# Three operations in place of four in each Newton round of the inverse root

## The reference

```
m = mean(x);  v = var(x)
layernorm(x) = (x - m) / sqrt(v + 1e-5)          # eight times
x = x + tanh(g) * part(layernorm(x), ...)
```

## Time and profile before

| | us |
|---|---|
| three timed executions | 1701.8, 1703.4, 1709.1 (median 1703.42) |
| the profiled execution | 1699.4 |
| its span, first to last instruction | 1697.6 |
| busy: PE, PE weight loads | 1273.9 (75%), 720.0 (42%) |
| busy: DVE | 1053.6 (62%), 2543 instructions |
| busy: ACT, POOL | 455.7 (27%), 330.9 (19%) |
| mean granted TensorE clock | 0.894 of full |

### The profile page before, as it was taken

The page is one execution under the profiler, slowest core; times in us unless marked ns, Lnnn a source line. Parts: engine busy times, 40 slices in busy tenths (PEclk is TensorE's granted clock), DMA queues, the critical chain, the costliest instruction groups (busy, mean ns, idle before and its releaser), DMA issues.

```text
span 1697.6 us, 20207 instructions
## 1 busy us (share of the span) xinstructions
PE 1273.9 (75%) x6670; PEld 720.0 (42%) x6670; DVE 1053.6 (62%) x2543; ACT 455.7 (27%) x632; POOL 330.9 (19%) x319
## 2 busy tenths in 40 slices
PE   0001799999979999867767635553899989899997
PEld 0000445445534456545445412222344545455554
DVE  8997545454434436657677788884788888833332
ACT  1124212222211323322222212221344445451110
POOL 2111000000004320004432342224333433100000
PEclk9996799999989999988987867656799999999999
DMA  9000000002000010011011000001322223200001
GB/s 309 13 12 12 1 0 0 0 0 102 0 19 1 0 62 0 1 25 26 0 25 25 1 19 0 0 0 42 98 77 86 77 77 90 59 2 0 0 0 49
DMA packets 67467, 55.68 MB, mean 33 GB/s; under 512 B 23888, under 2 KB 60624, under 8 KB 67152
## 3 DMA queue, kind: packets, MB, share of 16 engines
q1 hardware_dynamic: 66768, 54.67, 10.7%
q10 hardware_dynamic: 640, 0.26, 0.1%
HBM read 39.97 MB, written 14.68 MB: 32 GB/s over the span
## 4 chain that ended last, share of the span: by engine, by line
PE 59%; DVE 21%; issue 11%; POOL 4%; ACT 2%; DMA 1%; DVEq 1%; SPq 0%; POOLq 0%; ACTq 0%
PE banks L1994 7%; PE banks L1004 6%; PE banks L623 5%; PE banks L406 5%; PE banks L402 5%; PE banks L837 3%; PE banks L1011 3%; POOL sb_work L1429 3%; PE banks L829 3%; PE banks L413 3%; PE banks L417 2%; PE banks L1959 2%; DVE sb_work L317 2%; PE banks L1622 1%; DVE sb_work L1742 1%
## 5 line engine op out<-in xcount | busy, mean ns | idle before, releaser
L2232 DVE TENSOR_REDUCE sb_work<-banks 128x2 f32<-128x512 f32 x256 | 164.6, 685 | 51.3 <-PE banks L1959 49.2
L2103 ACT ACTIVATE sb_work<-banks 128x1024 f32<-128x1024 f32 x128 | 131.0, 1024 | 129.6 <-PE banks L1980 129.5
L523 DVE TENSOR_TENSOR sb_work<-sb_work,banks 128x512 f32<-128x512 f32 x72 | 49.4, 686 | 120.2 <-ACT sb_work L490 120.2
L1429 POOL TENSOR_TENSOR sb_work<-sb_work,sb_consts 128x512 f32<-128x512 f32 x64 | 66.6, 1071 | 265.5 <-ACT sb_work L1377 232.8
L1004 PE MATMUL banks<-sb_work,sb_shelf 128*128 128x512 f32 x256 | 114.4, 592 | 0.0
L406 PE MATMUL banks<-sb_work,sb_shelf 128*128 128x512 f32 (+1 forms) x192 | 88.8, 610 | 8.6 <-DVE sb_work L566 8.6
L623 PE MATMUL banks<-sb_work,sb_ctx_nat 128*64 128x512 f32 (+15 forms) x512 | 88.3, 503 | 7.8 <-DVE sb_work L685 7.8
L980 POOL TENSOR_TENSOR sb_late<-sb_w2n 128x1024 f32<-128x1024 f32 x10 | 22.7, 2269 | 366.7 <-DVE sb_work L677 366.1
L490 ACT ACTIVATE sb_work<-banks 128x512 f32<-128x512 f32 x72 | 42.9, 596 | 178.2 <-PE banks L402 116.2
L1083 DVE TENSOR_TENSOR sb_work<-sb_work,banks 128x512 f32<-128x512 f32 x32 | 22.0, 688 | 110.7 <-ACT sb_work L1069 110.7
L402 PE MATMUL banks<-sb_work,sb_shelf 128*128 128x512 f32 (+1 forms) x192 | 84.9, 593 | 0.0
(11 more groups left out here) (285 smaller groups left out, 2560.4 us busy)
## 6 DMA issues: line engine op xcount, KB each, us to landing
sb_work<-scratch SPq DMA_DIRECT2D x64, 192.0 KB
scratch<-sb_work SPq DMA_DIRECT2D x32, 192.0 KB, 2.1
sb_work<-ctx_t SPq DMA_DIRECT2D x16, 256.0 KB, 4.3
scratch<-sb_work SPq DMA_DIRECT2D x32, 128.0 KB, 2.1
sb_work<-ctx_t SPq DMA_DIRECT2D x4, 512.0 KB, 3.7
sb_ctx_nat<-ctx SPq DMA_DIRECT2D x1, 2048.0 KB, 11.2
sb_raw<-wguT SPq DMA_DIRECT2D x1, 2048.0 KB, 15.5
scratch<-sb_work SPq DMA_DIRECT2D x32, 64.0 KB, 1.8
```

What stands on the lines that cost most here:

```text
L1429: ins = nc.gpsimd.tensor_tensor(km_[:, hf, k, :, :], keys.unsqueeze(1).broadcast_to([P, 8, SEQ]), hm2.unsqueeze(2).broadcast_to([P, 8, SEQ ...
L2103: nc.scalar.activation(pt3[:, h % 2, :, :], o, ACT.Exp).then_inc(exp3, 1)
L2232: nc.vector.tensor_reduce(out=mx3[:, tc, k, 2 * hp:2 * hp + 2], in_=bank[u % 2].rearrange("p (h s) -> p h s", h=2), axis=AX, op=ALU.max).t ...
```

## The change

Each round of `rsqrt` computes the same value in three operations: t = (-0.5 * y) * y, t = t * v, y = (t + 1.5) * y. The first and the last are `scalar_tensor_tensor`, which takes a constant and two tensors. The numbers of links a round are changed to match, 18 to 15 and 16 to 13.

```diff
             for _ in range(3):
-                link(nc.vector.tensor_tensor(t, y, y, ALU.mult))
+                link(nc.vector.scalar_tensor_tensor(out=t, in0=y, scalar=-0.5, in1=y, op0=ALU.mult, op1=ALU.mult))
                 link(nc.vector.tensor_tensor(t, t, v, ALU.mult))
-                link(nc.vector.tensor_scalar(t, t, -0.5, 1.5, ALU.mult, ALU.add))
-                link(nc.vector.tensor_tensor(y, y, t, ALU.mult))
-
-        LN_LINKS = 18
+                link(nc.vector.scalar_tensor_tensor(out=y, in0=t, scalar=1.5, in1=y, op0=ALU.add, op1=ALU.mult))
+
+        LN_LINKS = 15
...
-                link.enter(b, 16 + LN_LINKS)
+                link.enter(b, 13 + LN_LINKS)
```

## The result

The changed kernel took 1697.40 us (median of 15 executions, 1690.5 to 1701.9) and the kernel before, beside it, 1706.56 us (15 executions, 1700.8 to 1712.4): a ratio of 0.9952, 95% interval 0.9935 to 0.9969. The change is a gain of 9.2 us where 14.0 were forecast from a median of 1703.4, so some 5 us are missing. The other 3.2 us between the forecast 1689.4 and the measured 1697.4 are the base: the kernel before, timed beside it, stood at 1706.6.

What follows compares the result with a forecast made beforehand. No one bound: the chain of waits spends 59% on PE and 21% on DVE. From the median 1703.4, less 10.7 us of path and 3.3 us of clock (14.0), it forecast 1689.4 us, range 1683 to 1697.

Steps and rivals of the forecast that it cites:

- The root's price: In every inverse root, fused operations at 0.193 us from start to start make three rounds 0.63 us shorter.
- Which 17 places pay: The norm ahead, wkv, bit, attn3 norms and ternary's root mean squares are on the path: 17 x 0.63 = 10.7 us.
- hidden places: The 20 norms off the path (moe, conv, ternary's norm, attn2, had): 12.6 us of DVE time hidden by PE or ScalarE.
- The waits: Predicted idle times: PE in ternary 1.6 us and in attn3 2.1 us, DVE in attn2 0.9 us.
- The clock term: In ternary, shorter PE waits remove two falls of the granted TensorE clock: 2 x 1.65 = 3.3 us gained.
- Where a stall goes, nothing new is late: In attn3 and ternary, PE's waits only shrink, 2.75 to 2.12 and 2.25 to 1.62 us, with no new delay.
- the changed counts cost nothing: The changed numbers of links are constants of a wait that is there anyway, so they add no time.
- (b): Ternary and attn3 give the gain back at the next wait; only nine places pay, 5.7 us, 1697.7 us; chance 0.12.
- (a): The path alone pays, 10.7 us; clock falls come elsewhere for those that go; 1692.7 us; chance 0.28.
- DVE's busy time: DVE's busy time over the whole kernel was to be lower by 19 to 21 us.
- rival (d): Slower: GpSimd holds the fused operation on DVE, 1.8 us a hold, 1723 us with one at each of 17; chance 0.03.

Runs made afterwards that it cites:

- again: The changed kernel itself run again with no edit, beside the kernel before: 1700.1 us, ratio 0.9954.
- again2: The changed kernel itself run once more with no edit, in a later comparison beside the kernel before: 1696.1 us, ratio 0.9933.
- pad42: The changed kernel with 42 idle wait instructions added to VectorE's stream in moe, no arithmetic changed: 1691.1 us, ratio to before 0.9922.
- pad16: The changed kernel with 16 idle wait instructions added to VectorE's stream in moe: 1691.3 us, ratio to before 0.9919.
- best16: The changed kernel with 16 idle wait instructions in VectorE's stream, a second run beside the unedited changed kernel: 1687.6 us, ratio to before 0.9884.
- path17: The kernel before with the new root only at the 17 places on the path, old form in the 20 others: 1691.9 us, ratio 0.9915.
- hidden20: The kernel before with the new root only in the 20 norms off the path, old form at the 17: 1706.6 us, ratio 0.9987.
- rounds4: The changed kernel with four Newton rounds in place of three at all 37 places: 1706.2 us, ratio to before 0.9983.
- rounds2: The changed kernel with two Newton rounds in place of three in every root: 1679.9 us, ratio to before 0.9847.
- pad128: The changed kernel with 128 idle wait instructions added to VectorE's stream in moe: 1705.5 us, ratio to before 0.9997.
- before_pad56: The kernel before (old root everywhere) with 56 idle wait instructions added to VectorE's stream in moe: 1716.4 us, ratio 1.0058.

## Why the prediction was wrong, step by step

To take the clock out, I fitted one line through the span of every timed execution against its mean granted clock, with one slope for all and a level for each kernel (60 executions of before, beside the eleven runs, and 108 of the others): 1.24 us of span less for each 0.001 of clock more, with 1.6 us of scatter left over. Clock that a change itself gives or takes is taken out with the rest. The levels against before at equal clock:

| kernel | clock | us against before, +- one error |
|---|---|---|
| before | 0.8904 | 0 |
| after / `again` / `again2` | 0.8931 / 0.8925 / 0.8940 | -5.7 / -4.0 / -6.6, +-0.5 to 0.7 |
| `pad42` / `pad16` / `best16` | 0.8939 / 0.8949 / 0.8963 | -10.9 / -9.7 / -10.8, +-0.6 to 0.7 |
| `path17` | 0.8938 | -10.1 +-0.7 |
| `hidden20`, `rounds4` | 0.8918, 0.8914 | -0.7 +-0.5 each |
| `rounds2` | 0.8955 | -19.4 +-0.7 |
| `pad128` | 0.8922 | +0.1 +-0.5 |
| `before_pad56` | 0.8868 | +3.9 +-0.5 |

And from one norm to the next in the profiles, us, worked out from the starts of the first operation of each norm:

```
             before  after  again2  pad42  path17  hidden20
wkv, 2nd      38.94  38.35  38.35   38.34  38.34   38.94
ternary 1st   31.87  31.28  31.40   31.27  31.35   31.89
ternary 2nd   33.52  31.23  31.22   31.22  31.23   33.53
bit, 2nd      43.75  40.82  40.78   40.87  40.81   41.45
bit, 3rd      43.76  40.88  40.88   40.91  40.89   43.78
had, 1st      42.16  42.15  42.16   42.16  42.16   42.15
attn3, 1st    76.73  75.57  75.97   75.57  75.56   76.49
attn3, 2nd    78.49  83.78  85.37   76.62   76.42   78.30
```

- **The root's price.** Right, with a small size off. A fused operation takes 163 ns, not 155, and 0.197 us from start to start, not 0.193; L151, from which it was taken, is shorter. A root saves 0.60 us in place of 0.63 (wkv 38.94 to 38.35), 17 of them 10.2 in place of 10.7.
- **Which 17 places pay.** Right. `path17` alone gives -10.1 at equal clock, `hidden20` -0.7; and `rounds2` takes another 8.5 to 9.7 off the kernels without the stall, where 17 x 0.59 = 10.0 was expected. The hidden places in had pay nothing (42.16 to 42.15).
- **The waits.** PE before L836 was idle for 1.65 (forecast 1.6), before L1967 2.13 (2.1), DVE before L1475 1.13 (0.9).
- **The clock term.** In ternary it is right. The falls behind the first and the third of its waits are there in all four profiles in which the root mean square has twelve operations (before, `hidden20`, `rounds4`, `before_pad56`; waits of 2.24 to 2.35 us) and in none of the nine in which it has fewer (waits of 1.74 us and less); ternary's 2nd row shows one of them, 33.5 to 31.2, of which 0.6 is the root. That is the forecast 3.3. As a sum over the kernel the equality is luck. (0.8931 - 0.8904) x 1237 = 3.3 us holds for after, but in the 21 executions without the stall (`pad42`, `pad16`, `best16`) the mean clock is 0.8950, worth 5.6 us. The prediction had no clock term for bit, and against the profile of before bit gave more than ternary: its 2nd and 3rd rows are 2.9 us shorter in all eight profiles with nine operations there. Of that 0.6 is the root and 2.3 goes with the clock, 4.6 for the two. The granted clock of one such stretch was 0.62 in before and 0.71 in after, PE's busy time 22.55 and 20.27:

```profile
1095.50:1139.30 43.80, 22.55 (x105) 12.00 (x106) 35.53 (x84) 9.83 (x13) 12.32 (x9) 0.62 0.00 0
```

```profile
1100.90:1141.80 40.90, 20.27 (x105) 11.20 (x106) 34.95 (x81) 9.94 (x13) 12.32 (x9) 0.71 0.00 0
```

  The old form gave 43.7 to 43.8 in before and `rounds4`, and either kind of block in `hidden20` and `before_pad56`, so the long blocks are not bound to it; why the 2nd and 3rd were short in all eight is not shown. In other parts falls come and go: from moe's first norm to the third it was 153.6 us in before and `pad42` and 156.8 to 157.0 in all the others.
- **The step that failed** is "Where a stall goes, nothing new is late", together with the sentence that the changed counts cost nothing: what a shorter stream does to the loading of the code was put at nothing without a reason. The change takes 87 instructions out of VectorE's stream, 72 of them ahead of attn3's loop, and that moved the loop to where its code has to be loaded again at its one turn back. Idle 5.5 to 5.7 us in place of 0.59 makes 4.9 to 5.1; the levels say the same, -5.5 for the mean of the 27 executions of after, `again` and `again2` and -10.4 for the 21 without the stall, a difference of 4.9. That is the stall at equal clock. As it is paid it is more: in all five profiles with it the granted clock is at 0.50 for the first 4 us that PE runs behind its wait, where the eight others show no fall, and attn3's 2nd row is 7.2 us longer in after than in `pad42`; the mean spans of the 27 and the 21 executions lie 7.1 us apart (1695.9 and 1688.8). None of my rivals had it. (b) came near in time (1697.7) and is wrong in mechanism, since attn3 and ternary pay in full where nothing stalls. (a) came nearer in difference, 10.7 forecast and 9.2 measured, and is wrong too, since ternary's falls did go.
- **The sum.** -10.2 (path) - 3.3 (clock) + 4.9 (stall) = -8.6 us; the mean spans of after and before lie 8.9 apart. Without the stall it is -10.2 - 5.6 = -15.8, and the 21 executions without it lie 16.0 below before. The 3.3 in the first sum is what is left of the 5.6 when the stall has taken some 2 back. So behind the missing 5 us stand a stall of some 7 as it is paid and a clock term some 2 above the forecast. By medians beside before, `pad16` is 14.1 us faster, `pad42` 14.3 and `best16` 19.1: without the stall the forecast of -14.0 would have held or been passed, with a clock term larger than it had.
- **DVE's busy time** was to fall by 19 to 21 us. It fell by 8.9 in after and by 18.7 in `again2` (1034.9). Most of the difference is another hold, of rival (d)'s kind though not of the fused operation (whose longest is 165 ns): in attn2 four tensor_scalar of L1109 took 3.50 us in place of 1.14 where the GpSimd product L1428 began beside them. After, then `again2`, in the second block:

```profile
866.90 3.50 DVE L1109 TENSOR_SCALAR sb_late<-sb_xn,sb_qr 128x256 f32<-128x256 f32 x4
...
867.09 4.22 POOL L1428 TENSOR_TENSOR sb_work<-sb_work,sb_consts 128x512 f32<-128x512 f32 x4 [24.36 <-ACT sb_work L1376]
```

```profile
865.61 1.14 DVE L1109 TENSOR_SCALAR sb_late<-sb_xn,sb_qr 128x256 f32<-128x256 f32 x4
...
867.38 4.05 POOL L1428 TENSOR_TENSOR sb_work<-sb_work,sb_consts 128x512 f32<-128x512 f32 x4 [25.96 <-ACT sb_work L1376]
```

  In the first the product begins 0.2 us after L1109, in the second L1109 has ended 0.6 us ahead of it. The Trainium skill, "SBUF — State Buffer", section "Who interferes with whom", has this contention of the two engines over a shared port pair as a full block, with which the rows agree. The caught pattern comes with blocks of 58.1 us in place of 54.6 and repeats over three blocks, some 10.5 us. It was there in after, `again`, `pad42` and `best16`, not in `again2`, `pad16`, `pad128` or `rounds2`, and not in before, `path17` or `rounds4`; in `hidden20` and `before_pad56` there was a trace of it (6.1 us for the sixteen such operations, where it is 4.6 without and 11.7 with the whole pattern). One program shows both, so it is a state that an execution falls into; whether the shorter norm makes it likelier stays open. It does not explain the missing 5 us: `pad42` and `best16` have it too and lie at -10.9 and -10.8 at equal clock, while `again2` has none of it and lies at -6.6. It may be part of the scatter from 1690.5 to 1701.9 us of after.

## What to carry to other kernels

Count an edit's instructions in the stream of its engine as well as its time: where a hardware loop's code just fits in what stays loaded, as the 299 instructions here, taking instructions out ahead of it can cost what eight of the places gained (4.9 us at 0.6 each), and more with the clock that falls behind the stall. "issue" idle behind a loop's branch, with instruction loads around it, is how it shows, and a few idle instructions under a long wait are a cheap way to test it and to cure it. For chained operations as small as these (128x4 f32) it is their number on the path that pays, at about 0.2 us each, in the forms tried here. Last, look for a clock term in every part where a wait gets shorter: here the part that was not looked at gave the most.

## What the runs showed of the hardware

- A turn of a hardware loop on VectorE left it idle for 0.59 us where the second round loaded no code, and for 5.5 to 5.7 us where it loaded again, for loops of 293 to 305 instructions; which of the two it was went with the loop's place modulo 128 instructions, over seven places, of which the two with the stall share one remainder.
- Behind that stall, in five profiles of five, the granted TensorE clock was 0.50 over the first 4 us of PE's work; the stall cost 4.9 us at equal clock and 7.1 by mean spans.
- A scalar_tensor_tensor on 128x4 f32 in a chain took 163 ns and 0.197 us from start to start, the tensor_tensor 162 ns and the same distance.
- 128 idle instructions (256 waits for a semaphore long up) kept VectorE for 12.7 us, some 0.1 us each.
- Two executions of one program can differ by 3.5 us a block in attn2, by whether a VectorE tensor_scalar is caught by a GpSimd product.
